# Half of an f32 matrix product in three float32r passes, its splits on ScalarE and GpSimd, and the first load on two queues

## The chip, the cores and the metric

The kernel runs on one core of one Trainium2 chip. The metric is the device time of one execution in microseconds. Engines are named PE (TensorE), DVE (VectorE), ACT (ScalarE), POOL (GpSimd) and SP (SyncE, which here only issues DMAs).

## The reference, cut to what matters

Twelve layers of attention without softmax over 16 batches of 256 tokens and 128 channels, then a LayerNorm, a gated FFN and a second LayerNorm.

```python
for i in range(12):
    q, k, v = split(x @ Wqkv[i].T + bqkv[i])         # 16 heads of 8 channels
    att = einsum('bhqd,bhkd->bhqk', q, k) / sqrt(8)  # no softmax
    y = einsum('bhqk,bhkd->bhqd', att, v)            # back to (B, T, C)
    x = y @ Wproj[i].T + bproj[i] + x
x = layernorm(x0 + x)
h = silu(x @ wg.T) * (x @ wu.T)                      # 384 hidden, int weights / 127
x = layernorm(x + h @ wd.T)
```

## The kernel before

Since nothing in a layer is nonlinear in the tokens, the kernel never touches them between the first and the last step. It forms each batch's 128x128 Gram matrix once (line 749, from the token tiles `xt`), and carries for each batch a matrix pair `state` through the layers. A layer multiplies the state by a batch's own matrix `step`. Each engine runs its own program, written out by hand, and the engines meet on semaphores.

The work of one layer on PE, in its order (16 batches in four groups of 4, g = 0 to 3; two halves of 8, h = 0 and 1):

- gk products (line 781), a row of means (807), their parts of m (792), m itself (800). ACT copies gk out (422). DVE multiplies m by a block mask into `mt` (563, `take_blocks`).
- s (line 820, `s_stage(0)`, `s_stage(1)`): `mt` times the projection weights. The result lies in four PSUM banks per half. ACT copies quads 0 and 1 of each half to `s_rows` (425) and DVE copies quads 2 and 3 (568, `take_s`).
- n (line 834, `n_stage(0)`, `n_stage(1)`): wq times s. For each of four quads i, four products with a contraction of 32 rows run on the four row groups k of the array, each into a PSUM bank of its own, 256 columns each. Operands are f32, and each f32 product appears in the trace as two MATMUL and two LDWEIGHTS instructions, so a half is 32 and a layer 64 of them.
- DVE adds the identity to n and writes `step` (574, `add_identity(0)` to `(3)`, two groups for each half).
- h (line 867): Gram matrix times `step`, four groups. Groups 0 and 1 wait until `step` of both is there, groups 2 and 3 likewise. Ahead of group 2 stands `shift_stage` (760), which needs `mbq`. DVE makes `mbq` from `bqp`, a product of `mt` and the query bias (584), by a reduction (588).
- u (lines 731 to 733, `three_pass`): `step` times state in float32r, hi times hi, hi times lo, lo times hi, for 8 pairs of batches. ACT makes the rounded hi parts (431 `step_hi`, 435 and 450 `state_hi`); POOL makes `step_lo` (350); DVE makes `state_lo` (609, 621). A hi part is a copy into a float32r tile, a lo part is the f32 value minus the hi part.

In the last layer the u part is left out. POOL sums `bsum` there (343), PE runs line 897 on it, and a pipelined FFN over 8 chunks of 512 tokens follows. Weights of a layer (`w`, two buffers) are loaded by SP two layers ahead, when `n_done` and `shift_ready` have passed.

At the start PE multiplies a tile of zeros 7 times (`WARM_START`, line 738, 14 instructions) and then waits for the token tiles, which come in 8 pairs (`x_in`): pairs 0, 2, 4, 6 on SP's queue, 1, 3, 5, 7 on ACT's.

Of the kernel before, what the change touches and what calls it, by code (L numbers as in the profile page):

```python
# [24 lines left out]
F32 = mybir.dt.float32  # L25
F32R = mybir.dt.float32r
# [5 lines left out]
P = 128  # L32
# [5 lines left out]
QUAD = 32  # L38
# [7 lines left out]
CT = 4  # L46
CHUNKS = TILES // CT
EPS = 1e-5
WARM_START = 7
LOW_LAYER = 2  # L50
SCALE_ATT = float(np.float32(1.0) / np.sqrt(np.float32(HEAD)))
SCALE_W = float(np.float32(1.0 / 127.0))
# [16 lines left out]
def build(nc, x_tok, x_chan, weights, ffn_weights, consts, out):  # L69
# [3 lines left out]
    with ExitStack() as ctx:  # L73
# [39 lines left out]
        step_hi = sb("step_hi", [P, BATCHES, P], F32R)  # L113
        step_lo = sb("step_lo", [P, BATCHES, P], F32R)
        step_hi_f = step_hi[:].bitcast(F32)
        s_rows = sb("s_rows", [P, 2, QUADS, 2 * P])
        gk = sb("gk", [P, BATCHES, P])
        mt = sb("mt", [P, BATCHES, QUAD])
        a_cent = sb("a_cent", [P, BATCHES, P])
# [50 lines left out]
        hid = xt_flat[:, half_cols:2 * half_cols].rearrange("p (j t) -> p j t", j=HC)  # L170
        nu_b = gram

        x_in = [sem(f"x_in{i}") for i in range(PAIRS)]
        xchan_in = sem("xchan_in")
        cst_in = sem("cst_in")
        fw_in = sem("fw_in")
# [29 lines left out]
        shift_done = sem("shift_done")  # L206
        shift_ready = sem("shift_ready")
        s_done = sem("s_done")
        s_low_half_ready = sem("s_low_half_ready")
        s_high_half_ready = sem("s_high_half_ready")  # L210
        n_done = sem("n_done")
        step_ready = sem("step_ready")
        step_hi_ready = sem("step_hi_ready")
# [80 lines left out]
        @block.sync  # L294
        def _(sp):
            per = TILES // PAIRS
            for i in range(0, PAIRS, 2):
                sp.dma_start(xt[:, per * i:per * (i + 1), :], x_v[:, per * i:per * (i + 1), :]).then_inc(x_in[i], 16)
            sp.dma_start(w[:, 0, :], weights[0]).then_inc(w_in[0], 16)
            sp.dma_start(cst[:, :], consts).then_inc(cst_in, 16)  # L300
            for i in range(1, PAIRS, 2):
                sp.wait_ge(x_in[i], 16)
            sp.dma_start(w[:, 1, :], weights[1]).then_inc(w_in[1], 16)
            sp.dma_start(fw_int[:, :], ffn_weights).then_inc(fw_in, 16)
            sp.dma_start(xchan[:, :], x_chan).then_inc(xchan_in, 16)

            for k in range(LAYERS - 2):
                sp.wait_ge(n_done, 2 * k + 2)
                sp.wait_ge(shift_ready, k + 1)
                sp.dma_start(w[:, k % 2, :], weights[k + 2]).then_inc(w_in[k % 2], 16)  # L310
            for c in range(CHUNKS - 1):
                sp.wait_ge(o_ready, c + 2)
                sp.dma_start(out_v[bass.ds(c, 1), :, :, :].rearrange("a p t c -> (a p) t c"),
                             o[:, bass.ds(c * (CT * P), CT * P)].rearrange("p (t c) -> p t c", t=CT)).then_inc(out_done, 16)
            for h in range(2):
                sp.wait_ge(o_ready, CHUNKS + 1 + h)
                sp.dma_start(out_v[CHUNKS - 1][:, halves[h], :],
                             o[:, (CHUNKS - 1) * CT * P:].rearrange("p (t c) -> p t c", t=CT)[:, halves[h], :]).then_inc(out_done, 16)
            sp.wait_ge(out_done, 16 * (CHUNKS + 1))
# [3 lines left out]
        def _(pool):  # L323
# [11 lines left out]

            def layer(s, at, last, first):

                if last:

                    pool.wait_ge(b_lo_ready, at(PAIRS, PAIRS))  # L340
                    pool.wait_ge(kdiag_ready, at(1, 1))
                    for g in range(GROUPS):
                        nc.gpsimd.tensor_tensor(group(bsum, g), state_hi_f[:, GB * g:GB * (g + 1), S_B:S_B + P],
                                                state_lo_f[:, GB * g:GB * (g + 1), S_B:S_B + P],
                                                ALU.add).then_inc(bsum_ready, 1)
                    return

                for g in range(GROUPS):
                    pool.wait_ge(step_hi_ready, at(GROUPS, g + 1))
                    nc.gpsimd.tensor_tensor(group(step_lo, g), group(step, g), group(step_hi_f, g),  # L350
                                            ALU.subtract).then_inc(step_lo_ready, 1)
                if at(1, 0) == 1:

                    pool.wait_ge(ffn_chain, 2)
                    nc.gpsimd.tensor_tensor(wgu_lo[:, :], fw[:, 0:2 * HIDDEN], wgu_hi[:, :].bitcast(F32),
                                            ALU.subtract).then_inc(ffn_w_ready, 1)
                    pool.wait_ge(xchan_in, 16)
                    pool.wait_ge(means_ready, 2)
                    centre(0, 0)
                    centre(1, 1)  # L360
# [44 lines left out]
        @block.scalar  # L405
        def _(act):
            per = TILES // PAIRS
            for i in range(1, PAIRS, 2):
                act.dma_start(xt[:, per * i:per * (i + 1), :], x_v[:, per * i:per * (i + 1), :]).then_inc(x_in[i], 16)

            act.wait_ge(warm_set, 1)
# [6 lines left out]
            def layer(s, at, last, first):  # L418

                for g in range(GROUPS):  # L420
                    act.wait_ge(gk_done, at(GROUPS, g + 1))
                    nc.scalar.copy(group(gk, g), products(GK_BANKS[g])).then_inc(gk_ready, 1)  # L422
                for h in range(2):
                    act.wait_ge(s_done, at(2, h + 1))
                    nc.scalar.copy(s_rows[:, h, 0:2, :], s_banks(h)[:, 0:2, :]).then_inc(s_low_half_ready, 1)  # L425
                if last:
                    return

# [72 lines left out]
        def _(dve):  # L501
# [19 lines left out]
            def layer(s, at, last, first):  # L521
# [41 lines left out]
                    nc.vector.tensor_tensor(group(mt, g), ps[:, M_BANKS[g], 0:P].rearrange("p (b i) -> p b i", b=GB),  # L563
                                            blk.unsqueeze(1).to_broadcast([P, GB, QUAD]), ALU.mult).then_inc(m_ready, 1)

                def take_s(h):
                    dve.wait_ge(s_done, at(2, h + 1))
                    nc.vector.tensor_copy(s_rows[:, h, 2:4, :], s_banks(h)[:, 2:4, :]).then_inc(s_high_half_ready, 1)  # L568

                def add_identity(g):  # L570
                    if g % 2 == 0:
# [5 lines left out]

                for g in range(GROUPS):
                    take_blocks(g)
                take_s(0)  # L580
                take_s(1)

                dve.wait_ge(m_ready, at(GROUPS, GROUPS))
                nc.vector.tensor_tensor(bqp[:, :, :], mt[:, :, :],
                                        w[:, s, BQ:BQ + QUAD].unsqueeze(1).to_broadcast([P, BATCHES, QUAD]),
                                        ALU.mult).then_inc(bqp_ready, 1)
                dve.wait_ge(bqp_ready, at(1, 1))
                nc.vector.tensor_reduce(mbq[:, :], bqp[:, :, :], AX_X, ALU.add).then_inc(mbq_ready, 1)
                for h in range(2):
                    add_identity(2 * h)  # L590
                    add_identity(2 * h + 1)

                def take_shift():
                    dve.wait_ge(shift_done, at(1, 1))
# [134 lines left out]
        def _(pe):  # L729
# [12 lines left out]


            for pair in range(PAIRS):
                pe.wait_ge(x_in[pair], 16)
                for k in range(2):
                    for part in range(2):
                        t = 2 * (2 * pair + k) + part
# [21 lines left out]
            def layer(s, at, last_layer, first):  # L770
# [55 lines left out]
                def n_stage(h):  # L826


                    pe.wait_ge(s_low_half_ready, at(2, h + 1))
                    pe.wait_ge(s_high_half_ready, at(2, h + 1))  # L830
                    for i in range(QUADS):
                        for k in range(QUADS):
                            r = slice(QUAD * k, QUAD * (k + 1))
                            last = nc.tensor.matmul(n_banks(h)[:, k, :], w[r, s, WQ + P * i:WQ + P * (i + 1)],  # L834
                                                    s_rows[r, h, i, :], start=i == 0, stop=i == QUADS - 1)
                    last.then_inc(n_done, 1)

                pe.wait_ge(w_in[s], at(8, 16 - 8 * s))
# [221 lines left out]
```

## Time and profile before

| | |
|---|---|
| median of 3 executions | 323.78 us (323.13 to 323.87) |
| profiled execution, its own time | 323.34 us |
| its span in the profile | 321.6 us |
| busy: PE, DVE, ACT, POOL | 309.2, 223.6, 182.6, 95.9 us |
| one layer | about 20.5 us |

The span is what the profile covers; 1.7 us of the execution lie around it. Busy time of PE comes from modelled ends of pipelined instructions, so the distance between starts tells more than the length of one. In the tables and rows L834 is line 834 of the kernel, PEld is the loading of weights into the array, "x64" counts instructions, and `32*128 32x256` is a product with 32 rows of contraction, 128 output rows and 256 columns.

### The profile page before, as it was taken

The numbers are of one execution on the slowest core, as the hardware profiler recorded it, in microseconds if no ns is written. First come the engines' busy times: TensorE is split into PE (matmuls) and PEld (weight loads), VectorE is DVE, ScalarE is ACT, GpSimd is POOL, SyncE is SP. The second block draws the span as 40 slices with busy tenths as digits, with TensorE's granted clock in tenths as the row PEclk, the third lists the DMA queues.
The fourth block names the chain that finished last, engine by engine and source line by source line (L and its number), as shares of the span: only waits on it lengthen the run. The fifth ranks groups of instructions, "written<-read, shape, count | busy, mean of one in ns | idle before, by whom it ended". The sixth has DMA issues, their size and how long they took to land.

```text
span 321.6 us, 9031 instructions
## 1 busy us (share of the span) xinstructions
PE 309.2 (96%) x3792; PEld 290.9 (90%) x3792; DVE 223.6 (70%) x638; ACT 182.6 (57%) x417; POOL 95.9 (30%) x89
## 2 busy tenths in 40 slices
PE   8999999999999999999999999999999999999992
PEld 8989899899898998989989899899998999999882
DVE  0367776875776757767677677676767668888873
ACT  2448757476584774846738557485573065444550
POOL 2005055060320602306014060050516052655442
PEclk9999999999999999999999999999999999999999
DMA  7842002020020200201002011020000000121112
GB/s 276 328 167 75 6 4 74 2 78 2 2 75 5 75 2 3 78 2 63 15 2 79 2 26 52 4 77 2 2 3 2 2 1 2 33 60 41 33 35 70
DMA packets 7594, 14.94 MB, mean 46 GB/s; under 512 B 512, under 2 KB 4736, under 8 KB 7424
## 3 DMA queue, kind: packets, MB, share of 16 engines
q1 hardware_dynamic: 6976, 13.27, 12.4%
q10 hardware_dynamic: 576, 1.06, 0.9%
q8 instruction: 32, 0.52, 0.7%
q14 instruction: 10, 0.08, 0.1%
HBM read 12.23 MB, written 2.10 MB: 45 GB/s over the span
## 4 chain that ended last, share of the span: by engine, by line
PE 93%; DVE 3%; DMA 1%; issue 1%; POOLq 0%; POOL 0%
PE ps L834 14%; PE ps L781 13%; PE ps L867 13%; PE ps L731 7%; PE ps L733 7%; PE ps L947 7%; PE ps L732 7%; PE ps L800 4%; PE ps L935 3%; PE ps L936 3%; PE ps L749 3%; DVE s_rows L568 3%; PE ps L820 3%; PE ps L913 2%; PE ps L807 2%; PE ps L792 2%
## 5 line engine op out<-in xcount | busy, mean ns | idle before, releaser
L350 POOL TENSOR_TENSOR step_lo<-step,step_hi 128x512 fp32r<-128x512 f32 x44 | 54.9, 1282 | 172.5 <-ACT step_hi L431 172.5
L731 PE MATMUL ps<-state_hi,step_hi 128*128 128x258 f32 x176 | 50.7, 288 | 0.0
L834 PE MATMUL ps<-s_rows,w 32*128 32x256 f32 x768 | 44.8, 381 | 5.2 <-DVE s_rows L568 5.2
L733 PE MATMUL ps<-state_hi,step_lo 128*128 128x258 f32 x176 | 49.9, 283 | 0.0
L732 PE MATMUL ps<-state_lo,step_hi 128*128 128x258 f32 x176 | 49.7, 282 | 0.0
L834 PEld LDWEIGHTS ps<-s_rows,w 32*128 32x128 f32 x768 | 40.4, 185 | 7.2 <-ACT s_rows L425 7.2
L431 ACT CAST step_hi<-step 128x512 fp32r<-128x512 f32 x44 | 27.0, 619 | 33.8 <-DVE step L574 33.8
L781 PE MATMUL ps<-w,gram 128*128 128x128 f32 x352 | 42.9, 275 | 0.0
L781 PEld LDWEIGHTS ps<-w,gram 128*128 128x128 f32 x352 | 42.0, 192 | 0.6
L867 PE MATMUL ps<-step,gram 128*128 128x128 f32 x320 | 40.6, 281 | 0.0
L867 PEld LDWEIGHTS ps<-step,gram 128*128 128x128 f32 x320 | 37.3, 192 | 3.3 <-DVE step L574 3.3
L609 DVE TENSOR_TENSOR state_lo<-ps,state_hi 128x512 fp32r<-128x512 f32 x44 | 30.5, 692 | 12.2 <-ACT state_hi L435 10.7
L422 ACT COPY gk<-ps 128x512 f32<-128x512 f32 x48 | 28.1, 589 | 18.4 <-PE ps L781 18.4
L449 ACT COPY gram<-ps 128x256 f32<-128x256 f32 x88 | 32.9, 374 | 6.7
L574 DVE TENSOR_TENSOR step<-ps,cst 128x512 f32<-128x512 f32 x48 | 30.9, 686 | 8.3 <-PE ps L834 8.3
L621 DVE TENSOR_TENSOR state_lo<-ps,state_hi 128x256 fp32r<-128x256 f32 x88 | 36.6, 415 | 0.0
L450 ACT CAST state_hi<-ps 128x256 fp32r<-128x256 f32 x88 | 33.6, 382 | 0.0
L732 PEld LDWEIGHTS ps<-state_lo,step_hi 128*128 128x128 f32 x176 | 33.5, 190 | 0.0
L731 PEld LDWEIGHTS ps<-state_hi,step_hi 128*128 128x128 f32 x176 | 33.3, 189 | 0.0
L733 PEld LDWEIGHTS ps<-state_hi,step_lo 128*128 128x128 f32 x176 | 33.2, 189 | 0.0
L435 ACT CAST state_hi<-ps 128x512 fp32r<-128x512 f32 x44 | 25.8, 587 | 6.3 <-PE ps L867 6.3
L617 DVE TENSOR_TENSOR means<-ps,shift 128x4 f32<-128x4 f32 x88 | 14.4, 163 | 18.6 <-ACT state_hi L450 18.3
(102 smaller groups left out, 493.9 us busy)
## 6 DMA issues: line engine op xcount, KB each, us to landing
w<-weights SPq DMA_DIRECT2D x12, 592.5 KB, 3.7
xchan<-x_chan SPq DMA_DIRECT2D x1, 2048.0 KB, 10.5
out<-xchan SPq DMA_DIRECT2D x7, 256.0 KB, 2.3
xt<-x_tok ACTq DMA_DIRECT2D x4, 258.0 KB, 5.5
xt<-x_tok SPq DMA_DIRECT2D x4, 258.0 KB, 5.0
fw_int<-ffn_weights SPq DMA_DIRECT2D x1, 576.0 KB, 4.8
out<-xchan SPq DMA_DIRECT2D x2, 128.0 KB, 2.5
cst<-consts SPq DMA_DIRECT2D x1, 146.5 KB, 7.0
```

Of the source, the lines that this page charges most:

```text
L350: nc.gpsimd.tensor_tensor(group(step_lo, g), group(step, g), group(step_hi_f, g), ALU.subtract).then_inc(step_lo_ready, 1)
L449: nc.scalar.copy(gram[:, 2 * e:2 * e + 2, :], ps[:, two, 0:P]).then_inc(gram_ready, 1)
L450: nc.scalar.copy(state_hi[:, 2 * e:2 * e + 2, S_B:S_B + P], ps[:, two, P:2 * P]).then_inc(b_hi_ready, 1)
L574: nc.vector.tensor_tensor(group(step, g), n_banks(g // 2)[:, :, P * j:P * (j + 1)], (project if last else ident).unsqueeze(1).to_broadcast ...
L609: nc.vector.tensor_tensor(state_lo[:, GB * g:GB * (g + 1), S_H:S_H + P], products(H_BANKS[g]), state_hi_f[:, GB * g:GB * (g + 1), S_H:S_H ...
L621: nc.vector.tensor_tensor(state_lo[:, 2 * e:2 * e + 2, S_B:S_B + P], ps[:, two, P:2 * P], state_hi_f[:, 2 * e:2 * e + 2, S_B:S_B + P], ALU ...
L731: nc.tensor.matmul(dst, l_hi, r_hi, start=True, stop=False)
L732: nc.tensor.matmul(dst, l_hi, r_lo, start=False, stop=False)
L733: return nc.tensor.matmul(dst, l_lo, r_hi, start=False, stop=True)
L781: last = nc.tensor.matmul(one_product(GK_BANKS[g], b), gram_raw[:, b, 0:P] if first else gram[:, b, :], w[:, s, WK:WK + P], start=True, st ...
L834: last = nc.tensor.matmul(n_banks(h)[:, k, :], w[r, s, WQ + P * i:WQ + P * (i + 1)], s_rows[r, h, i, :], start=i == 0, stop=i == QUADS - 1)
L867: last = nc.tensor.matmul(one_product(H_BANKS[g], b), gram_raw[:, b, 0:P] if first else gram[:, b, :], step[:, b, :], start=True, stop=True)
```

## The change

Of the product n, the second half (h = 1) is done in float32r: wq is split into `wq_hi` (a copy by ACT, ahead of its copies of s) and `wq_lo` (a subtraction by POOL), s of the second half into `s_hi` (ACT, two copies of two quads each) and `s_lo` (DVE, two subtractions). For each quad PE does three passes, hi times hi, hi times lo, lo times hi, each on four row groups: 48 instructions where there were 32. The first half stays as it was. `bqp` is made by POOL, and the reduction into `mbq` now stands between `add_identity(1)` and `add_identity(2)`. At the start `WARM_START` is 9, the first pair of token tiles is loaded in two halves, one on SP's and one on ACT's queue, and pairs 1, 3, 5, 7 go on SP's, 2, 4, 6 on ACT's.

```diff
 EPS = 1e-5
-WARM_START = 7
+WARM_START = 9
 LOW_LAYER = 2
...
         step_hi_f = step_hi[:].bitcast(F32)
-        s_rows = sb("s_rows", [P, 2, QUADS, 2 * P])
+        s_rows = sb("s_rows", [P, QUADS, 2 * P])
+        s_hi = sb("s_hi", [P, QUADS, 2 * P], F32R)
+        s_lo = sb("s_lo", [P, QUADS, 2 * P], F32R)
+        wq_hi = sb("wq_hi", [P, QUADS * P], F32R)
+        wq_lo = sb("wq_lo", [P, QUADS * P], F32R)
         gk = sb("gk", [P, BATCHES, P])
...
         x_in = [sem(f"x_in{i}") for i in range(PAIRS)]
+        x_first = slice(0, 2), slice(2, 4)
         xchan_in = sem("xchan_in")
...
             per = TILES // PAIRS
-            for i in range(0, PAIRS, 2):
+            sp.dma_start(xt[:, x_first[0], :], x_v[:, x_first[0], :]).then_inc(x_in[0], 16)
+            for i in range(1, PAIRS, 2):
                 sp.dma_start(xt[:, per * i:per * (i + 1), :], x_v[:, per * i:per * (i + 1), :]).then_inc(x_in[i], 16)
...
             sp.dma_start(cst[:, :], consts).then_inc(cst_in, 16)
-            for i in range(1, PAIRS, 2):
+            for i in range(2, PAIRS, 2):
                 sp.wait_ge(x_in[i], 16)
...
+                def low_of_wq():
+                    pool.wait_ge(wq_hi_ready, at(1, 1))
+                    nc.gpsimd.tensor_tensor(wq_lo[:, :], w[:, s, WQ:WQ + QUADS * P], wq_hi[:, :].bitcast(F32),
+                                            ALU.subtract).then_inc(wq_lo_ready, 1)
+                def bq_products():
+                    pool.wait_ge(m_ready, at(GROUPS, GROUPS))
+                    nc.gpsimd.tensor_tensor(bqp[:, :, :], mt[:, :, :],
+                                            w[:, s, BQ:BQ + QUAD].unsqueeze(1).to_broadcast([P, BATCHES, QUAD]),
+                                            ALU.mult).then_inc(bqp_ready, 1)
...
                                                 ALU.add).then_inc(bsum_ready, 1)
+                        if g == 1:
+                            low_of_wq()
+                    bq_products()
                     return
...
+                low_of_wq()
+                bq_products()
                 for g in range(GROUPS):
...
             per = TILES // PAIRS
-            for i in range(1, PAIRS, 2):
+            act.dma_start(xt[:, x_first[1], :], x_v[:, x_first[1], :]).then_inc(x_in[0], 16)
+            for i in range(2, PAIRS, 2):
                 act.dma_start(xt[:, per * i:per * (i + 1), :], x_v[:, per * i:per * (i + 1), :]).then_inc(x_in[i], 16)
...
                     nc.scalar.copy(group(gk, g), products(GK_BANKS[g])).then_inc(gk_ready, 1)
-                for h in range(2):
-                    act.wait_ge(s_done, at(2, h + 1))
-                    nc.scalar.copy(s_rows[:, h, 0:2, :], s_banks(h)[:, 0:2, :]).then_inc(s_low_half_ready, 1)
+                act.wait_ge(w_in[s], at(8, 16 - 8 * s))
+                if not first:
+                    act.wait_ge(n_done, at(2, 0))
+                nc.scalar.copy(wq_hi[:, :], w[:, s, WQ:WQ + QUADS * P]).then_inc(wq_hi_ready, 1)
+                act.wait_ge(s_done, at(2, 1))
+                nc.scalar.copy(s_rows[:, 0:2, :], s_banks(0)[:, 0:2, :]).then_inc(s_low_half_ready, 1)
+                act.wait_ge(s_done, at(2, 2))
+                for i in range(0, QUADS, 2):
+                    nc.scalar.copy(s_hi[:, i:i + 2, :], s_banks(1)[:, i:i + 2, :]).then_inc(s_hi_ready, 1)
                 if last:
...
-                def take_s(h):
-                    dve.wait_ge(s_done, at(2, h + 1))
-                    nc.vector.tensor_copy(s_rows[:, h, 2:4, :], s_banks(h)[:, 2:4, :]).then_inc(s_high_half_ready, 1)
+                def take_s():
+                    dve.wait_ge(s_done, at(2, 1))
+                    nc.vector.tensor_copy(s_rows[:, 2:4, :], s_banks(0)[:, 2:4, :]).then_inc(s_high_half_ready, 1)
+                def low_of_s(i):
+                    dve.wait_ge(s_hi_ready, at(2, i // 2 + 1))
+                    nc.vector.tensor_tensor(s_lo[:, i:i + 2, :], s_banks(1)[:, i:i + 2, :], s_hi[:, i:i + 2, :].bitcast(F32),
+                                            ALU.subtract).then_inc(s_lo_ready, 1)
...
                     take_blocks(g)
-                take_s(0)
-                take_s(1)
-                dve.wait_ge(m_ready, at(GROUPS, GROUPS))
-                nc.vector.tensor_tensor(bqp[:, :, :], mt[:, :, :],
-                                        w[:, s, BQ:BQ + QUAD].unsqueeze(1).to_broadcast([P, BATCHES, QUAD]),
-                                        ALU.mult).then_inc(bqp_ready, 1)
+                take_s()
+                low_of_s(0)
+                low_of_s(2)
+                add_identity(0)
+                add_identity(1)
                 dve.wait_ge(bqp_ready, at(1, 1))
                 nc.vector.tensor_reduce(mbq[:, :], bqp[:, :, :], AX_X, ALU.add).then_inc(mbq_ready, 1)
-                for h in range(2):
-                    add_identity(2 * h)
-                    add_identity(2 * h + 1)
+                add_identity(2)
+                add_identity(3)
...
             for pair in range(PAIRS):
-                pe.wait_ge(x_in[pair], 16)
+                pe.wait_ge(x_in[pair], 16 if pair else 32)
                 for k in range(2):
...
-                    pe.wait_ge(s_low_half_ready, at(2, h + 1))
-                    pe.wait_ge(s_high_half_ready, at(2, h + 1))
+                    if h == 0:
+                        pe.wait_ge(s_low_half_ready, at(1, 1))
+                        pe.wait_ge(s_high_half_ready, at(1, 1))
+                    else:
+                        pe.wait_ge(s_lo_ready, at(2, 2))
+                        pe.wait_ge(wq_lo_ready, at(1, 1))
                     for i in range(QUADS):
-                        for k in range(QUADS):
-                            r = slice(QUAD * k, QUAD * (k + 1))
-                            last = nc.tensor.matmul(n_banks(h)[:, k, :], w[r, s, WQ + P * i:WQ + P * (i + 1)],
-                                                    s_rows[r, h, i, :], start=i == 0, stop=i == QUADS - 1)
+                        quad = slice(P * i, P * (i + 1))
+                        f32 = w[:, s, WQ + P * i:WQ + P * (i + 1)]
+                        parts = ((wq_hi[:, quad], s_hi), (wq_hi[:, quad], s_lo), (wq_lo[:, quad], s_hi)) if h else ((f32, s_rows),)
+                        for p, (left, right) in enumerate(parts):
+                            for k in range(QUADS):
+                                r = slice(QUAD * k, QUAD * (k + 1))
+                                last = nc.tensor.matmul(n_banks(h)[:, k, :], left[r, :], right[r, i, :],
+                                                        start=i == 0 and p == 0, stop=i == QUADS - 1 and p == len(parts) - 1)
                     last.then_inc(n_done, 1)
```

## Rows read from the trace of the kernel before

**Rows 1.** Page, the chain that ended last: share of the span by engine.

```profile
PE 93%; DVE 3%; DMA 1%; issue 1%; POOLq 0%; POOL 0%
```

**Rows 2.** Chain of waits in order of time, fifth layer (start us, us, what).

```profile
81.10 0.70 DVE s_rows L568
...
81.94 3.73 PE ps L834 x64
...
87.79 1.88 PE ps L867 x16
89.67 0.12 PE ps L731
```

**Rows 3.** Timeline, 77.2 to 82.6 us (start us, us, what, [idle before it <- releaser]).

```profile
80.31 1.19 PE L820 MATMUL ps<-w,mt 32*128 32x128 f32 x32
81.10 1.07 ACT L425 COPY s_rows<-ps 128x512 f32<-128x512 f32 x2 [1.56 <-PE ps L820]
81.10 1.29 DVE L568 COPY s_rows<-ps 128x512 f32<-128x512 f32 x2 [0.38 <-PE ps L820]
81.91 0.77 PEld L834 LDWEIGHTS ps<-s_rows,w 32*128 32x128 f32 x16 [0.60 <-ACT s_rows L425]
...
82.31 0.68 DVE L584 TENSOR_TENSOR bqp<-mt,w 128x512 f32<-128x512 f32 x1
```

**Rows 4.** Timeline, 82.6 to 91.2 us.

```profile
82.23 3.44 PE L834 MATMUL ps<-s_rows,w 32*128 32x256 f32 x60
...
83.03 0.69 DVE L588 TENSOR_REDUCE mbq<-bqp 128x16 f32<-128x512 f32 x1
84.01 1.29 DVE L574 TENSOR_TENSOR step<-ps,cst 128x512 f32<-128x512 f32 x2 [0.30 <-PE ps L834]
...
85.43 5.00 POOL L350 TENSOR_TENSOR step_lo<-step,step_hi 128x512 fp32r<-128x512 f32 x4 [15.87 <-ACT step_hi L431]
...
85.61 2.05 PE L867 MATMUL ps<-step,gram 128*128 128x128 f32 x16
85.73 1.29 DVE L574 TENSOR_TENSOR step<-ps,cst 128x512 f32<-128x512 f32 x2 [0.44 <-PE ps L834]
...
87.64 2.03 PE L867 MATMUL ps<-step,gram 128*128 128x128 f32 x16
```

**Rows 5.** Groups by line and shape (busy us, mean ns of one | idle us before).

```profile
L350 POOL TENSOR_TENSOR step_lo<-step,step_hi 128x512 fp32r<-128x512 f32 x44 | 54.9, 1282 | 172.5 <-ACT step_hi L431 172.5
...
L609 DVE TENSOR_TENSOR state_lo<-ps,state_hi 128x512 fp32r<-128x512 f32 x44 | 30.5, 692 | 12.2 <-ACT state_hi L435 10.7
...
L431 ACT CAST step_hi<-step 128x512 fp32r<-128x512 f32 x44 | 27.0, 619 | 33.8 <-DVE step L574 33.8
L435 ACT CAST state_hi<-ps 128x512 fp32r<-128x512 f32 x44 | 25.8, 587 | 6.3 <-PE ps L867 6.3
```

**Rows 6.** Timeline, 241 to 252 us, the last layer.

```profile
242.19 4.98 POOL L343 TENSOR_TENSOR gram_raw<-state_hi,state_lo 128x512 f32<-128x512 f32 x4 [8.18 <-DVE kdiag L528]
...
245.21 1.29 DVE L568 COPY s_rows<-ps 128x512 f32<-128x512 f32 x2 [0.38 <-PE ps L820]
...
246.41 1.32 DVE L584 TENSOR_TENSOR bqp<-mt,w 128x512 f32<-128x512 f32 x1
...
248.37 1.28 DVE L574 TENSOR_TENSOR step<-ps,cst 128x512 f32<-128x512 f32 x2
...
251.79 0.47 PE L897 MATMUL ps<-step,gram_raw 128*128 128x128 f32 x2
```

**Rows 7.** Timeline, the first 21 us.

```profile
1.05 3.36 PE L738 MATMUL ps<-warm 128*128 128x128 f32 x14 [1.05 <-DVE warm L502]
...
4.49 8.30 PEld L749 LDWEIGHTS ps<-xt 128*128 128x128 f32 x64 [0.38 <-DMA xt<-x_tok]
...
10.44 1.23 DVE L505 CAST state_hi<-cst 128x2048 fp32r<-128x2048 f32 x1 [9.44 <-DMA cst<-consts]
```

**Rows 8.** Stretch: PE, PEld, DVE, ACT, POOL busy (count), granted clock, DMA share, GB/s.

```profile
4.49:6.70 2.21, 2.21 (x10) 2.21 (x11) 0.00 (x0) 0.16 (x2) 0.00 (x0) 1.00 1.05 401
```

More of the change, by code:

```diff
@@ L208, in build @@
         s_done = sem("s_done")
+        wq_hi_ready = sem("wq_hi_ready")
+        wq_lo_ready = sem("wq_lo_ready")
         s_low_half_ready = sem("s_low_half_ready")
         s_high_half_ready = sem("s_high_half_ready")
+        s_hi_ready = sem("s_hi_ready")
+        s_lo_ready = sem("s_lo_ready")
         n_done = sem("n_done")
```

## The prediction

> **What bounds the kernel now.** I read the page's chain that ended last first, then that chain in order of time for one layer, then the timeline of the engines around n, and last the last layer and the start. PE holds 93% of the chain [rows 1]. In the fifth layer (it begins at 74.9 us; its eleven fellows repeat it at about 20.5 us) the only step of the chain that isn't PE is DVE's copy of s at 81.10; behind it come n (3.73 us), h and u without a hole [rows 2]. A microsecond taken from PE is a microsecond gained only as long as DVE, ACT and POOL keep up, and what the change touches is exactly the stretch where DVE is close behind. So the question is which of the two ends last where h begins, at 85.61 [rows 4].
>
> **n itself: the price of a float32r rank.** I call the four instructions that run at once on the four row groups a rank. Sixty instructions, 15 ranks, take 3.44 us [rows 4], of which some 0.37 is the end of the last one and 0.05 the spread within it; 14 distances make up 3.02, so a rank of f32 costs 0.216. A half of n has 8 ranks, 1.73 us. The new second half has 4 quads x 3 passes = 12 ranks. No row shows a float32r product on 32 rows. Nearest is u, float32r with 258 columns on the whole array: 0.12 an instruction [rows 2], or 0.119 for 256 columns. Bounds: 0.108 from below, half an f32 rank, since h, f32 on the whole array, takes 1.88 us for 16 instructions of 128 columns [rows 2], twice as long a column as u; from above 0.216, if a float32r rank gained nothing over an f32 one. I take 0.119, because f32 ranks already show that the row groups overlap fully (32x128, half the columns: 32 instructions in 1.19 with the first start and the end in it, about 0.11 a rank [rows 3]), so the weight loads of a rank fit within 0.11. Twelve ranks then cost 1.43, which is 0.30 less than 1.73.
>
> The nearest thing the Trainium skill has speaks against this: "TensorE: Matmul & The Clock Gate" says in the section on LDWEIGHTS that a load goes by its columns whatever its rows, P / 1.2 ns, so 107 ns here by its figure, and in the section on the mechanism of packing that a load overlaps running products only where the row group differs. By that rule a rank would be load plus stream, about 0.21, and the half 2.6 us instead of 1.43. The rows at 128 columns, 0.11 a rank with the same loads, don't bear it out.
>
> **When the second half can begin.** It starts eight ranks into n: first rank 81.94, second 82.23, then seven more distances, 83.74. It now waits for `s_lo` and `wq_lo`.
> - ACT: the copy of s for half 0 at 81.10, the next one 0.48 later (two in 1.07 [rows 3], one being 0.59). `s_hi` has `state_hi`'s form, 0.59 [rows 5]: 81.58 to 82.17 and 82.06 to 82.65.
> - DVE: `take_s` 81.10 to 81.79. `low_of_s` is `state_lo`'s form, 0.69 [rows 5]: 82.21 to 82.90 and 82.81 to 83.50. With 0.1 of signalling `s_lo` is there at 83.60, against a slot at 83.74. Weights are loaded a rank ahead, so 0 to 0.15 may be lost; I take nothing, since the slack found below hides it.
> - `wq_hi`: ACT is idle for 1.56 us ahead of 81.10 [rows 3]. The copy, `step_hi`'s form, 0.62 [rows 5], lies there, 79.5 to 80.1. Its two new waits (weights, the n of the layer before) were met long before; behind it stand ACT's copies of s, which would slip if it ended after 81.10.
> - `wq_lo` and `bqp` on POOL: `step_lo`'s form costs 1.28 [rows 5], and its sums in the last layer 1.25 each [rows 6]; I take 1.28 for both: 80.2 to 81.5 and on to 82.8. POOL had been idle for 15.87 us ahead of 85.43 [rows 4], so `step_lo`, queued behind, does not move. DVE wants `bqp` at 85.2. If that cover were gone, each would cost its 1.28.
>
> DVE loses `take_s(1)` and `bqp` (0.69 and 0.68 [rows 3]) and gains two `low_of_s` (1.38): it is free at 83.50, and `add_identity(0)` starts at 84.01 as before, since the first half of n ends when it did.
>
> **When h can begin.** PE's side: before, n's ranks ended at 83.74 + 1.73 = 85.47 and h started 0.14 later, 85.61. Now 83.74 + 1.43 + 0.14 = 85.31. DVE's side: h group 0 waits for both `add_identity(0)` and `(1)`, which end at 84.01 + 1.29 = 85.30 [rows 4]; from DVE's first copy of s (81.10 + 0.69) to the weight load behind it at 81.91 it took 0.12 [rows 3], with two waits. h has one; between nothing and 0.12 I take 0.10: 85.40. DVE ends last. The gain is 0.21 of the 0.30, and the rest is a new wait of some 0.09 of PE for `step`. A rank may cost up to 0.127 before it matters at all, and at 0.144 nothing is left.
>
> **Is it given back?** The `mbq` reduction (0.69 [rows 4]) now stands ahead of `add_identity(2)`: 85.21 to 85.89, then 85.80 to 87.09, against 87.02 before. h group 2 started at 87.64 [rows 4] and wants to start at 87.43; `step` is there at 87.19, slack 0.24. ACT's `step_hi(2)` and the copies behind it slip by 0.06, and `state_lo` with them, but u's first pairs want them half a microsecond later. I cost this at nothing; had it no cover it would cost 0.07 a layer. Next late would be h group 2, if PE gained 0.24 more.
>
> The last layer is different. POOL's four sums run 4.98 us from 242.19 [rows 6]; `wq_lo` goes between the second and the third (+1.25), `bqp` behind the fourth, ready at 249.7. So DVE's reduction ends at 250.43, `add_identity(2)` and `(3)` at 251.63, and line 897's third group can start at 251.73 instead of 251.79 [rows 6]. Its first group gains more: `bqp` there took 1.32, beside POOL's work, against 0.68 in the fifth layer [rows 3], and held up `add_identity(0)` until 248.37 [rows 6]; it can now start at 248.11. What counts is the later: gain 0.06.
>
> **The start.** Fourteen warm instructions take 3.36 us and the x products begin at 4.49, when pair 0 has landed [rows 7]. Eighteen last 4 x 0.213 (3.36 less the end of 0.42 or so, over 13, is 0.22) longer: x begins at about 5.05, whatever the DMA does. So bringing pair 0 in earlier on two queues is hidden behind the two added warm products, and costs and brings nothing; the fifth load on SP puts w[0] and the constants some 0.5 later in the issue order, but they share full engines, and DVE had the constants at 10.44 [rows 7] with PE wanting w[0] at 12.8. The column of the granted clock reads 1.00 up to 6.7, yet only ten x products start in those 2.21 us [rows 8], 0.22 each, and all 64 loads take 8.30 us [rows 7], which leaves (8.30 - 2.21 - 0.19) / 54 = 0.11 for the others: the same form at half pace, so the first stretch ran at the lower of the two levels, 1.2 GHz, after PE had been busy from 1.05 with one hole of 0.1. If it rises at the same time, only 7.7 products are done by 6.7 instead of 10, and 2.3 x 0.112 = 0.25 us is lost. Bounds: 0.5 lost, if it rises later; 0.6 gained, if PE's unbroken work lets it rise by 5.05 (64 x 0.112 + 5.05 = 12.2 against 12.8).
>
> **The sum**, on the profiled execution's own 323.34: 11 x 0.21 + 0.06 - 0.25 = 2.1 us less, 321.2. That execution lies 0.44 under the median of the three; the median less 2.1 is 321.6, which is my forecast. A measurement of this kernel tells about 0.3%, 1 us, from no change.
>
> **The rivals.**
> - A: float32r ranks on row groups cost what f32 ranks do, 0.216, because loads or results of the four groups get in each other's way at the doubled pace. 12 x 0.216 - 1.73 = 0.86 a layer, 10.3 in all: 334. It decides from 0.144 a rank. For it: no row shows the form. Against it: 0.11 a rank with the same number of loads at 128 columns [rows 3]. The page's rule named above would come out here. 0.15. If the groups didn't overlap at all it would be 48 x 0.119 a half, some 48 us more; f32 ranks speak against it, and I leave it within these 0.15.
> - B: the gain is eaten. `s_lo` or `wq_lo` comes 0.3 late (an ACT copy or a DVE subtraction slowed by POOL's two new operations, as `bqp` was in the last layer), or a rank costs 0.14. Then 323 to 324. Against it: `take_s`, which reads PSUM as `low_of_s` does, took its usual 1.29 for two beside POOL's work in the last layer [rows 3, 6]. 0.15.
> - C: PE is the later side after all, DVE's signal faster than I take, and the clock rises early: 11 x 0.25 + 0.6, 320.4 or less. 0.08.
> - The forecast: 0.62, with a range of its own of 320.8 to 322.5 from the start's bounds and 0.05 a layer of signalling.
>
> Faster 0.70, same 0.15, slower 0.15. The range reaches from 320.2 (most of C) to 323.9 (B), which leaves out A and a little of C.
>
> **What the profile would show.** n 0.2 to 0.3 us shorter in the chain, with float32r ranks 0.119 apart in its second half; a hole of 0.05 to 0.15 ahead of h with `step` as its releaser; layers 20.3 us long; x products starting near 5.05; POOL busy some 30 us more. The prediction is wrong if ranks are 0.144 or more apart, if PE waits for `s_lo` ahead of the second half by over 0.2, or if h group 2 or u waits for DVE.

## The result and the profile after

The changed kernel takes 319.75 us (median; 319.24 to 320.92) against 323.55 for the kernel before, measured beside it: a ratio of 0.9895 with a 95% interval of 0.9871 to 0.9919. Forecast were 321.6 us and a range from 320.2. So it is faster, as forecast, but by 3.4 to 3.8 us instead of 2.1, and the median lies 0.45 us below the range.

The page of the changed kernel's profile, engine totals and the chain that ended last ([rows 1] has the latter of before):

```profile
PE 305.8 (96%) x3988; PEld 289.6 (91%) x3988; DVE 220.8 (69%) x638; ACT 194.0 (61%) x441; POOL 125.1 (39%) x113
...
PE 94%; DVE 3%; issue 1%; POOLq 0%; POOL 0%
```

PE still holds the chain. POOL is busy for 29 us more, ACT for 11 us more, and none of that shows in the chain. The chain in order of time for the fifth layer, against [rows 2] (n is now line 880, h is 913, u is 769 to 771):

```profile
79.98 0.70 DVE s_rows L603
80.68 0.14 issue
80.81 3.43 PE ps L880 x79
84.25 2.03 PE ps L913 x16
86.28 0.13 PE ps L798 x2
86.41 1.88 PE ps L913 x16
```

n takes 3.43 where it took 3.73. The timeline of the same stretch, against [rows 3, 4]:

```profile
80.81 1.96 PE L880 MATMUL ps<-s_rows,w 32*128 32x256 f32 x29 [0.44 <-DVE s_rows L603]
81.08 1.29 DVE L607 TENSOR_TENSOR s_lo<-ps,s_hi 128x512 fp32r<-128x512 f32 x2 [0.41 <-ACT s_hi L460]
...
82.43 0.46 PE L880 MATMUL ps<-s_hi,wq_hi 32*128 32x256 f32 x1
...
82.73 0.33 PE L880 MATMUL ps<-s_lo,wq_hi 32*128 32x256 f32 x4
82.74 0.23 PEld L880 LDWEIGHTS ps<-s_hi,wq_lo 32*128 32x128 f32 x4
82.85 0.33 PE L880 MATMUL ps<-s_hi,wq_lo 32*128 32x256 f32 x4
82.86 0.23 PEld L880 LDWEIGHTS ps<-s_hi,wq_hi 32*128 32x128 f32 x4
82.88 1.29 DVE L614 TENSOR_TENSOR step<-ps,cst 128x512 f32<-128x512 f32 x2 [0.51 <-PE ps L880]
82.97 0.33 PE L880 MATMUL ps<-s_hi,wq_hi 32*128 32x256 f32 x4
...
83.81 0.32 PE L880 MATMUL ps<-s_lo,wq_hi 32*128 32x256 f32 x4
...
83.93 0.32 PE L880 MATMUL ps<-s_hi,wq_lo 32*128 32x256 f32 x4
84.09 0.68 DVE L627 TENSOR_REDUCE mbq<-bqp 128x16 f32<-128x512 f32 x1
...
84.22 2.05 PE L913 MATMUL ps<-step,gram 128*128 128x128 f32 x16
...
84.68 1.28 DVE L614 TENSOR_TENSOR step<-ps,cst 128x512 f32<-128x512 f32 x2
```

Each "x4" of PE is a rank (the four products that run at once on the four row groups), and the starts 82.73, 82.85, 82.97 show one every 0.12 us. The weight loads of a rank (PEld, 82.74) begin as the rank before it begins (82.73). DVE's two identities run from 82.88 to 84.17, and h begins at 84.22, 0.05 later. From the start of n to the start of h it is 3.41 us, against 81.94 to 85.61, 3.67, before: 0.256 less a layer. Over eleven layers, from the first gk product (12.41; before 12.82) to that of the last layer (235.69; before 238.86), the trace gives 2.75. The spans of the two profiled executions differ by 3.49 us:

| part | before | after | gain |
|---|---|---|---|
| start, up to the first gk product | 12.82 | 12.41 | 0.41 |
| eleven layers | 226.04 | 223.28 | 2.75 |
| last layer and all behind it | 82.70 | 82.37 | 0.33 |

Behind the first gk product, then, the change is worth 3.1 us: 308.7 before, 305.7 after. The other profiles bear that out. The rest of the span is 308.4 to 309.1 in the four others below that have n in f32 throughout, and 305.6 to 305.7 in `after_again`, `n_only` and `one_pass`, which have the second half of n in float32r (`after_warm7`, with a stall told of below, has 306.9, and `pieces` 306.1).

The start, against [rows 7]:

```profile
1.05 4.21 PE L776 MATMUL ps<-warm 128*128 128x128 f32 x18 [1.05 <-DVE warm L537]
5.05 7.52 PE L787 MATMUL ps<-xt 128*128 128x129 f32 x64
```

x begins at 5.05 as forecast, but the 64 products take 7.52 instead of 8.49. After two of them, at 5.47, the granted clock rises from the lower level (1.2 GHz) to the full one (2.4 GHz), and the distance between two products falls from 0.21 to 0.11 us. In the profile of before that came at 6.76, after ten.

### The profile page after: what moved, and what is told of

The parts are those of the page before. It is cut to its first block, busy times and chain, and to the rows that moved or that the text cites. A ratio compares the mean times of both kernels' runs of the same rounds, so it can differ in the third digit from the quotient of the medians.

```text
span 318.1 us, 9482 instructions
## 1 busy us (share of the span) xinstructions
PE 305.8 (96%) x3988; PEld 289.6 (91%) x3988; DVE 220.8 (69%) x638; ACT 194.0 (61%) x441; POOL 125.1 (39%) x113
## 4 chain that ended last, share of the span: by engine, by line
PE 94%; DVE 3%; issue 1%; POOLq 0%; POOL 0%
PE ps L913 14%; PE ps L819 13%; PE ps L880 13%; PE ps L771 7%; PE ps L769 7%; PE ps L993 7%; PE ps L770 7%; PE ps L838 4%; PE ps L982 4%; PE ps L981 4%; DVE s_rows L603 3%; PE ps L858 3%; PE ps L787 2%; PE ps L959 2%; PE ps L845 2%; PE ps L830 2%
## 5 line engine op out<-in xcount | busy, mean ns | idle before, releaser
L352 POOL TENSOR_TENSOR wq_lo<-w,wq_hi 128x512 fp32r<-128x512 f32 x12 | 15.3, 1277 | 111.3 <-ACT wq_hi L455 111.3
L451 ACT COPY gk<-ps 128x512 f32<-128x512 f32 x48 | 28.1, 589 | 18.3 <-PE ps L819 18.3
L647 DVE TENSOR_TENSOR state_lo<-ps,state_hi 128x512 fp32r<-128x512 f32 x44 | 29.5, 690 | 9.7 <-ACT state_hi L470 8.2
L880 PE MATMUL ps<-s_rows,w 32*128 32x256 f32 x384 | 24.1, 386 | 5.3 <-DVE s_rows L603 5.3
L394 POOL TENSOR_TENSOR rstd<-ve,minus_half 128x4 f32<-128x4 f32 x15 | 15.2, 1012 | 35.3 <-DVE ve L694 35.3
L514 ACT ACTIVATE xt<-ps 128x512 f32<-128x512 f32 x24 | 13.5, 592 | 24.0 <-PE ps L982 24.0
```

What stands on the lines that cost most here:

```text
L647: nc.vector.tensor_tensor(state_lo[:, GB * g:GB * (g + 1), S_H:S_H + P], products(H_BANKS[g]), state_hi_f[:, GB * g:GB * (g + 1), S_H:S_H ...
L880: last = nc.tensor.matmul(n_banks(h)[:, k, :], left[r, :], right[r, i, :], start=i == 0 and p == 0, stop=i == QUADS - 1 and p == len(parts ...
```

## The experiments

All ratios are to the kernel before, measured beside each kernel.

| kernel | median | ratio, 95% interval |
|---|---|---|
| start_only | 323.11 | 0.9992, 0.9972 to 1.0012 |
| warm9_only | 323.07 | 0.9996, 0.9978 to 1.0014 |
| x_only | 322.75 | 0.9991, 0.9969 to 1.0014 |
| n_only | 320.51 | 0.9917, 0.9887 to 0.9948 |
| bq_only | 322.90 | 0.9989, 0.9970 to 1.0008 |
| after_again | 319.72 | 0.9897, 0.9873 to 0.9922 |
| after_warm7 | 320.35 | 0.9896, 0.9871 to 0.9921 |
| one_pass | 319.82 | 0.9886, 0.9856 to 0.9916 |
| four_pass | 325.46 | 1.0065, 1.0035 to 1.0095 |
| bq_dve | 325.73 | 1.0082, 1.0058 to 1.0105 |
| pieces | 319.59 | 0.9882, 0.9846 to 0.9919 |

### The start apart from n

Two theories stand here: either more unbroken work of PE raises the clock sooner (G), or the rise has nothing to do with it and was early by chance in one profile (P). `start_only` is the kernel before with this alone:

```diff
-WARM_START = 7
+WARM_START = 9
...
-            for i in range(0, PAIRS, 2):
+            sp.dma_start(xt[:, x_first[0], :], x_v[:, x_first[0], :]).then_inc(x_in[0], 16)
+            for i in range(1, PAIRS, 2):
...
-            for i in range(1, PAIRS, 2):
+            act.dma_start(xt[:, x_first[1], :], x_v[:, x_first[1], :]).then_inc(x_in[0], 16)
+            for i in range(2, PAIRS, 2):
...
```

`warm9_only` has the first line of it, `x_only` the rest, and `n_only` is the changed kernel without either.

> The kernel before with the start of the changed one alone: 9 warm products and the first x pair on two queues, n as it was. In the changed kernel the x products began at 5.05 us (before: 4.49) and still ended at 12.57 (before: 12.98). Theory G, that PE's unbroken work from 1.05 us on lets the clock rise earlier: x products end some 0.4 us earlier than in the kernel before, all else the same, and the time is 0.4 to 0.6 lower, about 323.0. Theory P, that the rise falls at a time which has nothing to do with this work and only happened to be early in the one profile: the median is 0.25 higher, about 323.8, and the end of the x products lies anywhere from 12.0 to 13.5.

> The kernel before with WARM_START 9 alone, x loads as they were. The pair landed before 4.49 us there, so with warm products until 5.05 PE's work is unbroken too. Theory G: the same as start_only, x products end near 12.6 and the time is 0.4 to 0.6 lower. Theory P: 0.25 higher. A third, that only the earlier landing counts: as the kernel before.

> The kernel before with the first x pair on two queues and 7 warm products. If the pair lands by 4.2 us, x products follow the warm ones without a hole, 0.3 us earlier than before. Theory G: the clock rises early too, x products end at 12.57 less 2 x 0.21 or later, and this is the fastest of the three starts, 0.6 to 0.9 under the kernel before. Theory P: 0.15 to 0.3 lower. If the pair lands no earlier than before: no change.

> The changed kernel with the start of the kernel before: 7 warm products, x pairs by turns on the two queues. The layers gave 0.256 us each in the profile of the changed kernel, 2.75 from the first gk product to that of the last layer, and the last layer 0.2. Theory G: 320.5, that is 3.0 under the kernel before and 0.5 above the changed one. Theory P: 320.3 or below, no slower than the changed kernel, which then owes nothing to its start.

None of the three starts can be told from the kernel before, and n alone is 0.8% faster. `n_only` met its expected 320.5, but its interval overlaps that of the changed kernel, so the medians don't decide between G and P. The start of `start_only`:

```profile
1.05 3.71 PE L741 MATMUL ps<-warm 128*128 128x128 f32 x18 [1.05 <-DVE warm L505]
4.60 7.38 PE L752 MATMUL ps<-xt 128*128 128x129 f32 x64
```

The same 18 warm instructions took 3.71 here and 4.21 in the changed kernel: the clock was up at 4.1, before the first x product.

### The changed kernel again, and with 7 warm products

`after_again` is the changed kernel without an edit. `after_warm7` keeps the pair on two queues:

```diff
-WARM_START = 9
+WARM_START = 7
```

> The changed kernel once more, unchanged, beside the others of this call. The place where the clock rises lay at 4.1, 5.5 and 6.0 us in three profiles with 9 warm products and at 6.4, 6.8 and 6.9 in three with 7. If the rise is tied to PE's unbroken work, this profile has it by 6.0 again; if it is not, it may lie anywhere from 4 to 7. The n part costs 3.0 us less than before by the layers of the two profiles; with a start worth nothing the ratio is 0.9907, about 320.2 where before takes 323.2. With a start worth 0.5 it is 0.989.

> The changed kernel with 7 warm products instead of 9, the first pair still on two queues. X products then begin at 4.20 without a hole. Theory P (rise not tied to the work): 0 to 0.3 lower than the changed kernel. Theory G (more unbroken work, earlier rise): the rise lies at 6.4 or later and the time is 0.3 to 0.6 higher.

Both came out at 0.990. The table has all profiles but that of `pieces`, which stands below, grouped by warm products and queues. "Clock up" is the time at which that trace records the rise of the granted clock; the distance between products falls from 0.21 to 0.11 us there. (In `bq_only` the rise falls into the hole ahead of the first x product.)

| kernel | warm products, queues of pair 0 | clock up | first x product | first gk product |
|---|---|---|---|---|
| start_only | 9, two | 4.11 | 4.60 | 11.81 |
| after_again | 9, two | 4.37 | 4.73 | 11.96 |
| four_pass | 9, two | 4.99 | 5.03 | 12.18 |
| after | 9, two | 5.47 | 5.05 | 12.41 |
| bq_dve | 9, two | 5.70 | 5.05 | 12.52 |
| warm9_only | 9, one | 6.03 | 5.05 | 12.68 |
| one_pass | 9, two | 6.81 | 5.05 | 13.05 |
| bq_only | 7, one | 4.24 | 4.52 | 11.77 |
| before | 7, one | 6.76 | 4.49 | 12.82 |
| n_only | 7, one | 6.90 | 4.63 | 12.96 |
| after_warm7 | 7, two | 5.74 | 4.20 | 12.10 |
| x_only | 7, two | 6.43 | 4.20 | 12.42 |

G falls: the clock was up at 4.24 with 7 warm products and at 6.81 with 9. In the seven profiles with 9, in all of which PE works without a break up to the x products, the rise spreads over 2.7 us, and the first gk product comes up to 1.24 later with it. `after` and `after_again` are one and the same kernel, with the rise at 5.47 and at 4.37. To compare starts with the rise at the same place, I move `one_pass` (9 products, rise at 6.81) by half of the distance between the rises, since products run at half pace until the rise. At 6.76 and 6.90, where the profiles with 7 products and one queue have 12.82 and 12.96, it would stand at 13.03 and 13.09. So the start of the changed kernel costs 0.1 to 0.2 us, near the 0.25 that the prediction took for a rise that stays where it is. Two queues with 7 products would gain by the same estimate: 12.42 at 6.43, where 9 would stand at about 12.86. The medians are too coarse to show either. The profile of the changed kernel had its rise 1.3 us before that of the kernel before, which brought 0.4 instead of a loss of 0.2.

By that estimate `after_warm7` should gain 0.4 over the changed kernel, and its median does not. In its profiled execution, the longest of its six, the first layer took the gain away:

```profile
19.28 1.13 PE L880 MATMUL ps<-s_rows,w 32*128 32x256 f32 x13 [0.44 <-DVE s_rows L603]
...
20.67 1.14 PE L880 MATMUL ps<-s_rows,w 32*128 32x256 f32 x16 [0.25 <-issue]
20.67 0.94 PEld L880 LDWEIGHTS ps<-s_rows,w 32*128 32x128 f32 x17 [0.65 <-issue]
```

PEld stood still for 0.65 us in the middle of n with "issue" as the cause: nothing in the profile was being waited for. From n to h it took 4.33 in that layer and 3.41 in the other ten. In `after_again` the same layer took 3.56. Whether the other five executions had such a stall isn't known.

### One pass and four

These ask which engine sets the start of h. `one_pass` leaves out the products with `s_lo` and `wq_lo` in the second half, `four_pass` adds `wq_lo` times `s_lo`:

```diff
-                        parts = ((wq_hi[:, quad], s_hi), (wq_hi[:, quad], s_lo), (wq_lo[:, quad], s_hi)) if h else ...
+                        parts = ((wq_hi[:, quad], s_hi),) if h else ...                              # one_pass
+                        parts = ((wq_hi[:, quad], s_hi), (wq_hi[:, quad], s_lo), (wq_lo[:, quad], s_hi), (wq_lo[:, quad], s_lo)) if h else ...  # four_pass
```

> The changed kernel with hi times hi alone in the second half of n: 4 ranks instead of 12, the products with s_lo and wq_lo left out, all splits and waits kept. PE is then 0.96 us sooner through n. Theory D, that h begins when DVE has both identities of the first half (84.170 in the fifth layer, PE 0.054 later): h begins 3.41 us after n as now, and the time changes by less than 0.5 in all. Theory E, that PE's 12 ranks set it: 0.96 x 12 = 11.5 us less.

> The changed kernel with a fourth pass, wq_lo times s_lo, in the second half of n: 16 ranks instead of 12. One pass instead of three changed nothing in the distance from n to h (3.41 us). If a rank costs 0.12 and PE was 0.04 ahead of DVE at h, h now begins 0.48 - 0.04 = 0.44 later in each layer: the distance is 3.85, and the time 12 x 0.44 = 5.3 us above the changed kernel, 325 against 319.7, so slower than f32. If the row groups had room to spare (a rank paced by something other than its columns), less.

Timeline of `one_pass`, fifth layer:

```profile
83.03 0.83 PE L880 MATMUL ps<-s_hi,wq_hi 32*128 32x256 f32 x15
83.44 1.29 DVE L614 TENSOR_TENSOR step<-ps,cst 128x512 f32<-128x512 f32 x2 [0.51 <-PE ps L880]
...
84.78 2.05 PE L913 MATMUL ps<-step,gram 128*128 128x128 f32 x16 [0.93 <-DVE step L614]
```

PE was done with n and stood idle for 0.93 us until the end of DVE's second identity (83.44 + 1.29 = 84.73), and h began 0.05 after it. From n to h it is 3.41, as in the changed kernel (3.409 against 3.411 in the mean of eleven layers). Theory D holds: a whole 0.96 us of PE's work is worth nothing there. The chain of `four_pass`:

```profile
81.03 0.70 DVE s_rows L603
81.74 0.14 issue
81.87 3.92 PE ps L880 x95
85.79 1.98 PE ps L913 x16
```

Four more ranks move h by 0.43 us a layer (3.84), where 0.44 was expected: a rank is 0.12, and PE in the changed kernel was 0.04 to 0.05 ahead of DVE. The kernel is then slower than in f32, 1.0065.

### bq

`bq_only` moves `bqp` to POOL and its reduction behind `add_identity(1)` in the kernel before:

```diff
+                bq_products()                    # POOL: the same tensor_tensor, behind m_ready
...
-                dve.wait_ge(m_ready, at(GROUPS, GROUPS))
-                nc.vector.tensor_tensor(bqp[:, :, :], mt[:, :, :],
-                                        w[:, s, BQ:BQ + QUAD].unsqueeze(1).to_broadcast([P, BATCHES, QUAD]),
-                                        ALU.mult).then_inc(bqp_ready, 1)
+                add_identity(0)
+                add_identity(1)
...
-                for h in range(2):
-                    add_identity(2 * h)
-                    add_identity(2 * h + 1)
+                add_identity(2)
+                add_identity(3)
```

`bq_dve` takes `bqp` back to DVE in the changed kernel:

```diff
                 add_identity(1)
+                dve.wait_ge(m_ready, at(GROUPS, GROUPS))
+                nc.vector.tensor_tensor(bqp[:, :, :], mt[:, :, :],
+                                        w[:, s, BQ:BQ + QUAD].unsqueeze(1).to_broadcast([P, BATCHES, QUAD]),
+                                        ALU.mult).then_inc(bqp_ready, 1)
                 dve.wait_ge(bqp_ready, at(1, 1))
```

> The kernel before with the bq part alone: bqp on GpSimd, its reduction between add_identity(1) and add_identity(2), n in f32 throughout, start as before. DVE was not what h waited for (its first identity began when n's first half was done), so eleven layers stay as they are; in the last one add_identity(0) no longer waits behind the 1.32 us of bqp: 0 to 0.25 less. Expected 0.1 less in all, not measurable. The rival, that DVE's order alone brings part of the 0.256 a layer: 1 to 3 us less.

> The changed kernel with bqp back on DVE, between add_identity(1) and the reduction (0.68 us). Identities of the second half then end 0.60 later, at 86.56 in the fifth layer, where h group 2 starts at 86.26. Prediction's reading (a slack of 0.24 to 0.25 ahead of h group 2): h group 2 is 0.36 late in each layer, 4.3 us in all, so 324. If PE's wait for step there had more room: no change. If everything DVE does shows up: 12 x 0.6 = 7.2.

`bq_only` is as the kernel before, 3.666 from n to h in each of the first eleven layers: the order of DVE alone brings nothing there. In the last one it takes 3.67 instead of 3.75. The chain of `bq_dve`:

```profile
82.16 2.04 PE ps L876 x32
...
84.23 1.29 DVE step L606 x2
85.52 0.61 DVE bqp L619
...
86.15 0.69 DVE mbq L623
86.83 1.21 DVE step L606 x2
...
88.08 2.05 PE ps L909 x16
```

Here DVE takes over the chain for 3.8 us. h begins on time, 3.41 after n, but its group 2 begins 5.93 after n instead of 5.44, so it is 0.48 late in each layer, where 0.36 was expected. The slack of 0.24 ahead of it was there; it is the identities that end later than expected, 5.87 after n instead of 5.14, which is 0.73 and not 0.60. The expectation had left out that the reduction now waits for DVE's own `bqp`: it begins 0.04 behind its end (86.11, 86.15), whereas in the changed kernel it begins 0.08 ahead of the end of the identity before it (84.09, 84.17). The time came out at 325.7, not 324. So `bqp` on POOL is what keeps the gain; n in float32r with it on DVE, in this place, is slower than the kernel before. Another place for it in DVE's order, between its copy of s and `low_of_s`, was not tried.

### The 2 MB of xchan in four pieces

`pieces` is `after_warm7` with this:

```diff
-            sp.dma_start(xchan[:, :], x_chan).then_inc(xchan_in, 16)
...
                 sp.dma_start(w[:, k % 2, :], weights[k + 2]).then_inc(w_in[k % 2], 16)
+                if k < 4:
+                    piece = slice(k * BATCHES * T // 4, (k + 1) * BATCHES * T // 4)
+                    sp.dma_start(xchan[:, piece], x_chan[:, piece]).then_inc(xchan_rest if k else xchan_in, 16)
...
+            pool.wait_ge(xchan_rest, 48)
```

> The changed kernel with 7 warm products and with the 2 MB of xchan loaded in four pieces behind the weights of layers 2 to 5, instead of in one transfer that fills the DMA engines until 21 us. In two of five profiles of kernels with the n part PE stood still in the first layer's n (0.15 and 0.92 us) with nothing that it waited for, while that transfer ran and PE's instructions were being fetched. If the two are connected, the first layer's distance from n to h is 3.41 here, and the median 0.2 to 0.6 lower than the changed kernel's, some 319.3. If not, a stall may stand elsewhere and the time is the same. Either way under what five rounds surely tell.

The first layer took 3.409 from n to h and the median is 319.59, 0.9882: not to be told from 0.9895. One profile without a stall, beside three with the large transfer that had none either, shows no cause. The trace of `after_warm7` even speaks against the transfer: this is the busy share of its DMA engines in tenths, 40 slices from 15 to 24 us.

```profile
DMA  9999689199695390000000000000003000000000
```

From about 18.4 us on the engines were less than a tenth busy, the transfer had landed by 19.27, and the hole in PE's work lay at 20.04 to 20.67, when nothing was being moved. Nor does an instruction fetch lie in the hole: the trace has two of 16 KB nearby, at 18.3 to 19.3 and at 21.9 to 23.3. So the stall didn't come while that transfer ran, as the expectation has it. In `after_again` the transfer landed only at 21.65, and there the loss of 0.15 came at 20.76 to 20.92, where three of the four row groups fell behind the first, with the DMA engines about a tenth busy. The cause of both stays open. The start of `pieces` had another surprise:

```profile
4.20 3.10 PE L791 MATMUL ps<-xt 128*128 128x129 f32 x24
...
7.65 4.73 PE L791 MATMUL ps<-xt 128*128 128x129 f32 x40 [0.36 <-DMA xt<-x_tok]
```

With x begun at 4.20 and the clock up at 4.71, PE ran out of x pairs and waited for a DMA; the first gk product came at 12.22, no earlier than with 9 warm products (12.18 in `four_pass`, clock up at 4.99). The gain of an earlier start ends where the loads do.

## Why the prediction was right and wrong

- **The rank, 0.119 forecast: right.** 0.12 in the timeline, and 0.43 for four of them in `four_pass`. Rival A is refuted: the loads of a rank begin as the rank before it starts, on the same row groups, and add no time of their own. The rule of the Trainium skill that was weighed ("TensorE: Matmul & The Clock Gate", on LDWEIGHTS and on the mechanism of packing), taken as load plus stream, would have given 0.21 by its figure, an estimate that this trace refutes. The same section on packing also lets a load run ahead of running products when it goes to a background weight buffer; the trace agrees with that sentence, though it doesn't show the buffer.
- **`s_lo`, `wq_hi`, `wq_lo` in time: right.** The second half started without a hole. `s_hi` took 0.60, `s_lo` 0.69, `wq_hi` 0.62, `wq_lo` 1.28, `bqp` on POOL 1.19 in the mean of twelve.
- **DVE ends last at h: right**, as `one_pass` shows by leaving out PE work at no gain. **Its size was off, and this is the step that failed in the layers.** The prediction put 0.10 between DVE's end and PE's start, from a row of 0.12 with two waits. It measured 0.055, in the fifth layer (84.17 to 84.22) and, with PE idle ahead of h, in all eleven layers of `one_pass`. With two waits PE's product begins 0.147 behind DVE's end, in all twelve layers at n and, in the last one, at h too (246.38 against 246.23). There the trace has the second wait as an instruction of its own on PE, 0.05 long, which stands between DVE's end and the weight load. So the number of waits makes the difference of 0.09, and taking off 0.02 for one of them was too little. 11 x 0.045 = 0.5 us, of which 0.44 is left in the sum of the eleven layers (2.75 against 11 x 0.21).
- **Not given back in the layers: right**, and so is the slack of 0.24 ahead of h group 2, as `bq_dve` shows (its identities end 0.73 later and group 2 begins 0.48 later).
- **The last layer, 0.06: too small.** From n to the third group of line 943 it took 5.54 us (242.88 to 248.42), before 5.75, a gain of 0.21. The term mis-sized is `bqp` on POOL, taken at 1.28; it took 1.12 there, and the reduction that waits for it and everything behind that come this much earlier:

```profile
245.23 1.12 POOL L357 TENSOR_TENSOR bqp<-mt,w 128x512 f32<-128x512 f32 x1
...
246.38 2.02 PE L943 MATMUL ps<-step,gram_raw 128*128 128x128 f32 x16
246.39 0.69 DVE L627 TENSOR_REDUCE mbq<-bqp 128x16 f32<-128x512 f32 x1 [0.15 <-POOL bqp L357]
246.99 1.28 DVE L614 TENSOR_TENSOR step<-ps,cst 128x512 f32<-128x512 f32 x2
```

- **The start, a loss of 0.25: this step failed too.** Two added products do cost 0.1 to 0.2 where the rise of the clock lies at the same place. But the rise lay anywhere between 4.1 and 6.9 us, with 7 warm products as with 9, and the prediction read one profile's 6.76, nearly the latest seen, as the place where it is. The two profiles had 6.76 and 5.47, so the start gained 0.41 where a loss of 0.25 was forecast: 0.66 us against the forecast. That part of the gap is the luck of two executions, not a gain of the change.

Together: 0.44 for the layers, 0.15 for the last one and 0.66 for the start. That is 1.25 of the 1.37 by which the profiled pair (3.49 us apart) exceeds 2.12; the other 0.12 lies mainly behind the last layer's third group and is not explained. The medians of the changed kernel and of the one before lie 3.8 and, in `after_again`, 3.6 apart, and 2.7 with n alone. The intervals overlap, and whether the start is worth something in the median stays open (`start_only`: 0.9992, plus or minus 0.2%). What is firm is that the layers and the end were forecast 0.7 us too low (2.37, measured 3.1); what the start adds to a median is not shown. The range failed at its lower end because a faster signal and an early clock together were counted only in rival C, with 0.08. Both were in the profiled execution. What else C says, that PE ends last at h, was not: DVE does, by 0.05.

## What to carry to other kernels

A pass saved on the engine that holds the chain is worth only the distance to the engine behind it: find that distance first, by leaving work out (one pass) and adding some (four), since here 8 ranks less were worth nothing and 4 more cost 0.43 of their 0.48 us. Take the signalling time from a row with the same number of waits, since it is multiplied by the layers. Never read the place of a clock rise from a single profile: here the start was up to 1.2 us longer or shorter with it from one kernel's profile to the next, and 0.45 us between two profiles of the same kernel, as much as any change of the start was worth.

## What the runs showed of the hardware

Float32r products with 32 rows of contraction on four row groups, into four PSUM banks, ran at 256 columns every 0.12 us for all four together, against 0.216 for f32, and their weight loads added nothing. PE's product began 0.055 us behind the end of the DVE operation that it waited for, and 0.147 where it waited for a second semaphore too. The clock's rise came at 4.1 to 6.9 us in thirteen profiles, with 7 warm products (4.2 to 6.9) as with 9 (4.1 to 6.8). PE stood still in the first layer's n with nothing to wait for in two of the five profiles of kernels with three passes and the 2 MB transfer: the layer took 0.92 longer in `after_warm7`, where the transfer was over by then, and 0.15 in `after_again`. The cause was not shown.
